# Edge tiles of 128 records in place of 125, their scatters dealt anew over the stages, and four fills issued later

## What is computed

```python
x = x + L0_gnn(xn, edges, type) + L0_mix(xn)      # attention over edges; 4 dense layers of linear attention and ffn
x = x + L0_ffn(layernorm(x))                      # 16 experts, two for each token
x = x + L1_gnn(xn, src, dst, w, w2) + L1_mix(xn)  # below; channel attention
x = x + L1_ffn(xn)                                # the gate picks rows
# in L1_gnn:
a_in  = segment_sum(feat_in[src] * iw[:, None], dst)
a_out = segment_sum(feat_out[dst] * ow[:, None], src)
```

## Time and profile before

| what | us |
|---|---|
| median of 3 runs | 5154.09 |
| lowest and highest run | 5144.35, 5155.28 |
| span of the profiled execution | 5104.5 |
| POOL busy with scatters (L737, 800 of them) | 1684.5 |

### The profile page before, as it was taken

The page is one execution under the profiler, slowest core; times in us unless marked ns, Lnnn a source line. Parts: engine busy times, 40 slices in busy tenths (PEclk is TensorE's granted clock), DMA queues, the critical chain, the costliest instruction groups (busy, mean ns, idle before and its releaser), DMA issues. The chain is left out here.

```text
span 5104.5 us, 67642 instructions
## 1 busy us (share of the span) xinstructions
PE 4208.8 (82%) x19715; PEld 3144.9 (62%) x19715; DVE 3215.8 (63%) x6298; ACT 2149.0 (42%) x7759; POOL 3136.1 (61%) x2100
## 2 busy tenths in 40 slices
PE   6779689889786688888888788469983999999998
PEld 4567467667564466666666566345552788887566
DVE  7667376576386888888888688731114444444447
ACT  2732463473281466666666588312221222222122
POOL 2013388787788777777777688688876445443300
PEclk9989889989898798988888899769996999999999
DMA  9999832332233788888888344449984565563100
GB/s 301 294 336 321 268 67 38 42 63 37 28 61 53 223 265 266 264 267 265 265 266 253 70 94 94 111 105 289 292 246 143 218 236 222 219 234 128 39 15 26
DMA packets 758155, 896.70 MB, mean 176 GB/s; under 512 B 382262, under 2 KB 617430, under 8 KB 754514
## 3 DMA queue, kind: packets, MB, share of 16 engines
q1 hardware_dynamic: 327060, 611.62, 36.0%
q0 software_dynamic: 411376, 263.90, 23.8%
q10 hardware_dynamic: 19406, 17.44, 1.1%
HBM read 668.38 MB, written 222.64 MB: 175 GB/s over the span
## 5 line engine op out<-in xcount | busy, mean ns | idle before, releaser
L737 POOL DMA_INDIRECT pairs<-REC,FARC x800 | 1684.5, 2106 | 619.6 <-DMA pairs<-REC,FARC 231.1
L1102 PE MATMUL a_pa<-a_VW,identf 128*128 128x260 f32 x1760 | 551.3, 468 | 207.9 <-issue 114.2
L994 POOL DMA_INDIRECT a_KV<-kv_tab,KEYS x556 | 536.5, 965 | 173.6 <-issue 159.1
L1102 PEld LDWEIGHTS a_pa<-a_VW,identf 128*128 128x128 f32 x1760 | 389.3, 232 | 289.8 <-issue 121.4
L2664 DVE TENSOR_TENSOR AIN<-AIN,w_pin 128x512 f32<-128x512 f32 (+1 forms) x325 | 216.6, 666 | 374.2 <-PE w_pin L2701 374.0
L1065 ACT ACTIVATE a_VW<-a_KV,a_VW 128x64 f32<-128x64 f32 x1668 | 407.3, 334 | 2.7
L994 POOL DMA_INDIRECT XN<-kv_tab,KEYS x324 | 312.7, 965 | 98.7 <-issue 90.2
L2709 PE MATMUL w_pout<-XN,w_tT 128*128 128x256 f32 x1250 | 318.7, 379 | 0.0
L2678 ACT ACTIVATE w_tT<-w_pt 128x256 f32<-128x256 f32 (+1 forms) x300 | 117.4, 391 | 457.8 <-PE w_pt L2696 456.1
L2599 POOL TENSOR_TENSOR RES<-RES,REC 128x1600 f32<-128x1600 f32 x52 | 188.0, 3631 | 187.6 <-DMA REC<-pairs 187.4
L2599 POOL TENSOR_TENSOR HB<-HB,REC 128x1600 f32<-128x1600 f32 x48 | 174.2, 3642 | 181.4 <-DMA REC<-pairs 181.0
(11 more groups left out here) (661 smaller groups left out, 10066.9 us busy)
## 6 DMA issues: line engine op xcount, KB each, us to landing
pairs<-ZERO SPq DMA_DIRECT2D x32, 5000.0 KB, 46.5
e_W<-in_L_ffn_w SPq DMA_DIRECT2D x192, 512.0 KB, 6.0
REC<-pairs SPq DMA_DIRECT2D x100, 800.0 KB, 8.0
RES<-pairs SPq DMA_DIRECT2D x13, 3200.0 KB
HB<-pairs SPq DMA_DIRECT2D x12, 3200.0 KB, 10.3
m_crow<-cell_tab SPq DMA_DIRECT2D x71, 488.3 KB
row_tab<-a_arow SPq DMA_DIRECT2D x220, 130.0 KB, 4.4
a_tyb<-ty_tab SPq DMA_DIRECT2D x110, 256.0 KB, 7.0
```

Of the source, the lines that this page charges most:

```text
L737: pool.indirect_dma_start(self.pairs[half], bass.IndirectOffsetOnAxis(self.FARC[:, i:i + 1].bitcast(I32), 0), self.REC[:, i, 0:4].bitcast( ...
L994: pool.indirect_dma_start(KV[t % UB][:, j, :], None, self.kv_tab, bass.IndirectOffsetOnAxis(self.SIDX[:, t * ROW + j:t * ROW + j + 1], 0)) ...
L1102: last = pe.matmul(sums[t % NA], self.identf[:, :], VW[:, t % NV, e, :, :], start=e == 0, stop=e == ROW - 1)
```

## The change

- Tiles have 128 records: EP = 128, 781 full columns and a tail of 32 edges in column 782 (EW = 781, EU = 782), padded to EC = 784 columns. The padding points at far cells and weighs zero. 98 merges in place of 100, histogram blocks of 28 columns (14 of them) in place of 40 (10), constants of the comparison and of the far cells to match. Each input is loaded by a DMA for the full columns and one for the tail, the latter after VectorE's memsets of the last columns.
- 782 scatters in place of 800, dealt as layers (32, 130, 260, 210), project 50, nodes 100, experts what is left (2), and none in att_out, route and batch_norm. (As layer 0's loop is written, its 32 come to 30 in both kernels.)
- The first 120 go to table 0 alone, in place of 40.
- In layer 1 the four fills are issued after the wait for cx, the weights and the next front, ahead of the back's cell loads.

```diff
-EP = 125
-EC = E // EP
+EP = P
+EW = E // EP
+EU = -(-E // EP)
+EC = -(-EU // 8) * 8
+FARNODE, FARSRC = 4032, 3199
-BESIDE = (32, 142, 150, 70)
+BESIDE = (32, 130, 260, 210)
-BACKS = ((3, 3, 3, 3, 2), (3, 3, 3, 3, 3), (3, 3, 3, 3, 3), ())
-ALONE = 40
-NODES = 156
-LAST = 14
+BACKS = ((3, 3, 3, 3, 2), (3, 3, 3, 3, 2), (3, 3, 3, 3, 2), ())
+ALONE = 120
+NODES = 100
+LAST = 0
...
-        HC, HL, HH = 40, 64, N // 64 + 1
+        HC, HL, HH = 28, 64, N // 64 + 1
...
+                    for x, empty in ((DI, FARNODE), (SI, FARSRC), (TI, 0)):
+                        dve.memset(x[:, EW:], empty)
+                    dve.memset(WT[:, :, EW:], 0.0).then_inc(s_pad, 1)
...
-                        act.dma_start(dst[0:EP, 0:EC], a[x].rearrange("(p e) -> p e", p=EP)).then_inc(s_in, 16)
+                        act.dma_start(dst[:, 0:EW], a[x][0:EP * EW].rearrange("(p e) -> p e", p=EP)).then_inc(s_in, 16)
+                    act.wait_ge(s_pad, 1)
+                    for dst, x in ((DI, "dst"), (SI, "src"), (TI, "edge_type_64")):
+                        act.dma_start(dst[0:E - EP * EW, EW:EW + 1], a[x][EP * EW:].rearrange("(p e) -> p e", e=1)).then_inc(s_in, 16)
...
-            if self.placed < EC:
+            if self.placed < EU:
...
-                    self.place_pairs(pool, 44)
+                    self.place_pairs(pool, 50)
...
-                    self.place_pairs(pool, 9)
...
-                    self.place_pairs(pool, 12)
...
-                            if layer == 1:
-                                self.fill(sp, 2 * FILL - LATE, 2 * FILL)
...
+                            if layer == 1:
+                                self.fill(sp, 2 * FILL - LATE, 2 * FILL)
...
-                    self.place_pairs(pool, 38)
```

More of the change, by code:

```diff
@@ L406, in open_up @@
         s_oh, s_hs, s_cnt, s_hd = (n(f"q_{x}") for x in ("oh", "hs", "cnt", "hd"))
-        s_p0, s_w1, s_p1, s_bo, s_own = (n(f"q_{x}") for x in ("p0", "w1", "p1", "bo", "own"))
+        s_p0, s_w1, s_p1, s_bo, s_own, s_pad = (n(f"q_{x}") for x in ("p0", "w1", "p1", "bo", "own", "pad"))
         s_cf, s_ct, s_cr, s_cd, s_park, s_rec = (n(f"q_{x}") for x in ("cf", "ct", "cr", "cd", "park", "rec"))
-        HC, HL, HH = 40, 64, N // 64 + 1
+        HC, HL, HH = 28, 64, N // 64 + 1
         NB = EC // (2 * HC)
@@ L449, in _ @@
                     pool.iota(PI[:, :], pattern=[[0, 1]], base=0, channel_multiplier=1).then_inc(s_io, 1)
-                    pool.iota(CPI[:, :], pattern=[[1, 2]], base=249, channel_multiplier=-2).then_inc(s_io, 1)
+                    pool.iota(CPI[:, :], pattern=[[1, 2]], base=490, channel_multiplier=-3).then_inc(s_io, 1)
                     v = self.bd[:, :].rearrange("p (h d) -> p h d", d=32)
@@ L456, in _ @@
                                        base=31, pattern=[[32, P // 32], [0, 32]], channel_multiplier=-1)
-                    pool.memset(self.REC[:, :, 7:8], 2.0 ** 121)
+                    pool.memset(self.REC[:, :, 7:8], 2.0 ** 119)
                     pool.memset(CNT[:, HH:], 0.0)
@@ L477, in _ @@
                     dve.wait_ge(s_io, 5)
-                    dve.tensor_scalar(CPI[:, :], CPI[:, :], 23, None, ALU.logical_shift_left)
+                    dve.tensor_scalar(CPI[:, :], CPI[:, :], 22, None, ALU.logical_shift_left)
                     for j in range(LOW):
@@ L482, in _ @@
                     dve.drain()
-                    dve.tensor_scalar(self.C2[:, :], CPI[:, 0:1].bitcast(F32), 1.5, None, ALU.mult).then_inc(s_cp, 1)
+                    dve.tensor_scalar(self.C2[:, :], CPI[:, 0:1].bitcast(F32), 2.0, None, ALU.mult).then_inc(s_cp, 1)
                     dve.tensor_scalar(SG[:, :], SGI[:, :], -2.0, 1.0, ALU.mult, ALU.add)
@@ L488, in _ @@
                     dve.tensor_tensor(SP[:, 1:], SG[:, 0:LOW - 1], SG[:, 1:], ALU.mult)
-                    dve.wait_ge(s_in, 48)
+                    dve.wait_ge(s_in, 96)
                     live = lambda x: x[0:EP, 0:EC]
@@ L506, in _ @@
                         dve.tensor_tensor(oht[:, b % 2, :, :, :], high.unsqueeze(2).to_broadcast([EP, 2, HH, HC]), ior[:, 0:HH, :].unsqueeze(1).to_broadcast([EP, 2, HH, HC]), ALU.is_equal).then_inc(s_oh, 1)
-                        if b == 2:
+                        if b == 3:
                             dve.wait_ge(x_in, 32)
@@ L512, in _ @@
                             self.finish_stats(dve, st, mean[:, :], var[:, :], NT).then_inc(x_st, 1)
-                        elif b == 3:
+                        elif b == 4:
                             dve.wait_ge(x_sd, 1)
@@ L522, in _ @@
                                                   ALU.subtract, ALU.mult).then_inc(x_xn, 1)
-                        elif b == 5:
+                        elif b == 7:
                             dve.wait_ge(s_p0, 1)
                             dve.tensor_tensor(WR[:, :, :], WT[:, :, :], parts[0], ALU.subtract).then_inc(s_w1, 1)
-                        elif b == 7:
+                        elif b == 10:
                             dve.wait_ge(s_p1, 1)
@@ L574, in _ @@
                     self.load_back(act, 0)
-                    act.wait_ge(s_pin, 32)
+                    act.wait_ge(s_pin, 64)
                     act.activation(parts[0], WT[:, :, :], ACT.Copy).then_inc(s_p0, 1)
@@ L2280, in experts @@
         XU, XR = 4, 8
-        LEFT = EC - self.placed - LAST
+        LEFT = EU - self.placed - LAST
         with ExitStack() as c:
@@ L2479, in _ @@
                 def _(pool):
-                    self.place_pairs(pool, EC - self.placed)
+                    self.place_pairs(pool, EU - self.placed)
                     self.wait_pairs(pool)
@@ L3017, in run @@
         self.ty_tab, self.dl_tab = self.dram("ty_tab", [P * SW], BF16), self.dram("dl_tab", [P * SW // ROW], BF16)
-        self.pairs, self.cell_tab = [self.dram(f"pairs{h}", [CELLS + E, 2]) for h in range(2)], self.dram("cell_tab", [EC, EP])
+        self.pairs, self.cell_tab = [self.dram(f"pairs{h}", [CELLS + EP * EC, 2]) for h in range(2)], self.dram("cell_tab", [EC, EP])
         self.xn_tab = self.dram("xn_tab", [NP, D])
@@ L3024, in run @@
         table = ExitStack()
-        RECS = self.sb(table, "REC", [P, EC, 8], BF16)
-        self.REC, self.FARC = RECS[0:EP, :, :], self.sb(table, "FARC", [EP, EC])
+        RECS = self.sb(table, "REC", [P, NP // 4, 8], BF16)
+        self.REC, self.FARC = RECS[:, 0:EC, :], self.sb(table, "FARC", [EP, EC])
         self.PART = RECS[:, :, :].rearrange("p e j -> p (e j)").bitcast(F32).rearrange("p (b n) -> p b n", b=2)
```

3 lines of the change are left out of this document (2 added, 1 removed).

## The result

The changed kernel takes 5361.66 us in the median (5353.56 to 5375.85), the kernel before 5152.97 beside it: a ratio of 1.0421, 95% interval 1.0396 to 1.0447, 209 us slower. The forecast was 5119, with a range of 5060 to 5240.

A forecast was written before the change was run, and what follows sets the result against it. The prediction saw POOL near its limit, though not alone, in layers 1 to 3, nodes and experts. Its terms, -22 - 20 + 38 - 22 - 7 - 2 = -35, took the median 5154.1 to 5119 us, range 5060 to 5240.

The forecast's parts named there:

- the term of the scatter's price: POOL's scatter of 128 records: busy 0.74 us, period p = 1.04 with issue, between plain DMA and gather.
- +38: Layer 3, 70 scatters become 210: at p = 1.04 the layer takes 218.4 us against 180.7.
- -20: Layer 2, 150 scatters become 260: covered up to p = 1.46, so POOL's tail of 21.4 us goes.
- the other sign that the text named: Prediction also wrong if scatters wait for their table's former pair to land; such waits were 71.3 us in layer 1.
- its bound of 1.21 for the turn: Layer 3: from p = 1.21 on, 210 p - 180.7 reaches the 73 us gained elsewhere.
- The rival with POOL as the bound of the layers: Scatter costs the gather's price or more, POOL bounds layer 3: 5167 at p = 1.27, some 5275 at 1.6; chance 0.21.
- the unchanged price of 2.50: Rival for layers 2 and 3: tiles of 128 leave the scatter's period at 2.50 us, total 5695; chance 0.14.
- Layer 1, -22: Fills moved on SP: VectorE's 27.5 us wait for m_crow goes, 5 charged for later back loads.
- Experts, -22: Experts lose all but 2 scatters; of TensorE's 36.3 us waits for e_XS, 8.0 and 6 stay.
- Opening and layer 0, -7: Tiles of 128: 4 us off the wait for edge types, 3 off layer 0's waits for m_crow.
- Merges, -2: Two merges fewer save some 2.5 us of VectorE each, part of it covered: -2 us.
- stages at 0: Project and nodes not ended by POOL; att_out, route and batch_norm, which lose scatters, covered by VectorE's chain: 0 us.

The follow-up runs named there:

- tiles alone: The changed kernel with the deal, ALONE and place of the fills taken back, so only tiles of 128 stay: 5395.06 against 5542.44 us, ratio 0.9741.
- deal alone: The kernel before with only the new deal and ALONE = 120, tiles still of 125: 6161.36 against 5542.44 us, ratio 1.1119.
- fills alone: The kernel before with the four fills issued after the wait for cx and ALONE left at 40: 5641.65 us, ratio 1.0187.
- first deal by the price: The changed kernel with 140, 170, 76 scatters in layers 1 to 3, 180 in nodes, 14 in batch_norm: 5399.00 us, ratio 0.9747.
- the two fill runs: The kernel before with the four fills after the wait for cx, with ALONE = 40 (5641.65 us, ratio 1.0187) and ALONE = 120 (5660.48, ratio 1.0191).

## Why the prediction was wrong

**The step that failed** is "I take the middle of the plain DMA and the gather, busy 0.74, p = 1.04", the term of the scatter's price. It measured 1.54, and 1.93 to 1.99 apart with the stalls. Put into the prediction's own formula, the layers come out: layer 3 405.1 - 180.7 = +224 in place of +38 (the stage: +227), layer 2 517.1 - 400.5 = +117 in place of -20 (the stage: +116). The waits of pairs for their landing, the other sign that the text named, were 5.7 and 0.6 us in these two layers, so they are not the cause. The mechanism was the one that the text named as deciding, and its bound of 1.21 for the turn, with the cover of 1.46 for layer 2, was passed by far. The rival with POOL as the bound of the layers was the right kind; it was priced up to a period of 1.6, at 5275, and the period of 1.93 to 1.99 lay beyond it, short of the unchanged price of 2.50.

Why the middle was wrong: both ends of it were DMAs that don't add, and the plain write of 128 records shows what the addition costs, 0.57 us. The argument against a low price, that a scatter that adds must read, add and write, stood in the text and got no weight. That POOL's DMAs with a list of 128 cost "at most 1.02" was read from medians and means: single gathers took up to 1.38 us, and a fourth kind, 50 gathers of 0.955, was left out; neither moves the sum. The comparison "125 costs twice what a gather of 128 costs" mixed two differences, the addition and the divisor; only one of them changed. The Trainium skill's rule by the divisor was cited there, for the loads alone; the page gives it for DMAs issued from GpSimd too, and so it bore on the one term that decided, though it has no price.

**Layer 1, -22**: -29 (and -40 between the later profiles). The wait of 27.5 us went, and 12.6 came back where 5 had been charged. But that the stage came out near the forecast is in part luck, for the tiles alone, with the fills still at the head of the queue, make layer 1 397 us long, nearly as short as the changed kernel's 394. VectorE's wait there was:

```profile
DVE m_same L1656 <- DMA m_crow<-cell_tab: 19.8, 1, 19.8
```

Four runs of chip 12 part the two effects. From POOL's first scatter of layer 1 to VectorE's last row it took, in us:

| | fills at the head | fills late |
|---|---|---|
| tiles of 125 | 414.5 (deal alone) | 389.3 (fills alone) |
| tiles of 128 | 393.5 (tiles alone) | 373.5 (first deal by the price) |

The four deals differ too, so this parts them only roughly, and on chip 3 the move took off 14 (416.8 in the kernel before, 403.2 with late fills and ALONE = 120). Still, the move of the fills takes 14 to 25 us off VectorE's time, about as forecast, and the tiles take off another 16 to 21, for which the sum had 2 us of merges. Part of the two together was lost on POOL. The cover of the scatter that needs table 1 held (it is number 122, not 120, and went out at 849.8, long after the fills), but POOL ended the layer 6 us after VectorE, since its pairs waited 137 us for landings. Nine of these waits, from 659 to 745, while the moved fills run, take 4.3 to 8.4 us each, 62 us in all, against 1.7 to 2.7 after the fills:

```profile
692.31 1.54 POOL L747 DMA_INDIRECT pairs<-REC,FARC  x1 [8.21 <-DMA pairs<-REC,FARC]
...
754.90 1.54 POOL L747 DMA_INDIRECT pairs<-REC,FARC  x1 [1.71 <-DMA pairs<-REC,FARC]
```

That the late fills need a long ALONE, and that a long ALONE brings these waits, the two fill runs show.

**Experts, -22**: -38. The mechanism was right, but TensorE's wait for e_XS fell to 6.5, not 14. The first wait was all that stayed. The rest of the gain, some 8 us, goes with TensorE's own busy time, which fell from 387 to 376 us at a granted clock of 0.99 in place of 0.96; the sum had no term for it. The tiles alone give most of it too (9.8 us of such waits with 117 scatters there), as does the deal alone (6.5 us): at 1.84 apart two scatters and a gather fit under a tile, and with hardly any scatters a gather does.

**Opening and layer 0, -7**: -19. The types' wait went from 12.1 to 1.8, so ScalarE's table was not what followed. By the rule of the Trainium skill ("DMA: Bandwidth & Descriptors", "How many engines (k)") both this wait and layer 0's for m_crow should shrink; the first did, by 85%. The second grew in this pair of profiles, 27.9 to 34.9 us, but on chip 12 it is 25.4 and 26.7 us in two kernels of 125 and 21.3 and 20.9 in two of 128, on chip 8 34.5 against 30.7 to 33.6, and on chip 3 29.1 and 38.3 against 36.7, so it shrank on two chips and the third can't say. Layer 0 itself is 13 to 17 us shorter with tiles of 128 on chips 12, 3 and 8, where this pair has 4.

**Merges, -2, and stages at 0**: these can't be told apart from the rest in the layers; in the tiles' run layers 2 and 3 are both shorter than the cover that the prediction took (369 us from POOL's first scatter to VectorE's end in layer 2, not 379, and 160 in layer 3, not 164). Project, nodes and route gained 2 to 5 us each. Batch_norm, counted at 0 with "if it weren't, these would be gains", lost 13 us in the first pair and 4 in the second. The overlap of its subtractions with GpSimd's additions came with the deal, but what it costs differs from one profile to the other, and the tiles alone, with 14 scatters ahead of the additions and subtractions of 419 ns, have a batch_norm of 81 us: there the additions meet VectorE's later steps, two of which take 2504 ns each in place of 288.

**The sum against the median.** The 49.6 us between span and median were taken to lie outside the span. In the changed kernel's profiled execution only 1.7 us do (5368.88 against 5367.2). With as much, the profiled execution of the kernel before took some 5106 us, 38 less than the lowest of its four runs (5144 to 5155), but as much as its runs on chip 2 (5096 to 5119). So it may come from another chip than the runs; the record doesn't say. This leaves the forecast difference as it is, but the first table by stages adds up to 54 us more than the medians show, and its small rows, layer 0's above all, are less sure than the two large ones.

What stays open: layer 0's time goes with the chip (tiles of 128: 391 to 392 us on chips 12 and 2, 405 to 409 on chips 8 and 3 and in the first comparison; tiles of 125: 405 to 406 on chip 12, 422 to 425 on chips 8 and 3, 412 in the first profile), and no run shows why; nor what makes the attention stage long on chips 12, 8 and 3.

## What to carry to other kernels

Before you fill a stage with cheaper work, find the price at which it stops being covered (here 210 p = 180.7 less what the rest gains, p = 1.21), and if no row shows that operation, take the bound on the wrong side of it seriously, not a middle between rows of other operations. Two operations that differ in two ways, as this scatter and gather do, bound nothing between them until one way is held fixed. And when a deal is written by hand, time one part alone: the tiles were worth 147 us, and the deal gave away more than all of it.

## What the hardware showed

- An adding scatter of 127 records of 8 bytes holds POOL 4.70 us, one of 128 1.54, one of 64 1.42, one of 128 without the addition 0.97.
- VectorE's tensor_tensor in fp32 slows when GpSimd runs one at the same time, but not always the same engine: 951 ns in place of 418 in the changed kernel's first profile, while in its second, on chip 8, VectorE kept 425 ns and GpSimd's two additions took 12.87 us in place of 7.37.
- POOL stands idle 1.7 to 2.7 us for the landing of the pair of adding scatters before, and 4.3 to 8.4 while fills of 5 MB run (changed kernel, layer 1).
- The same attention stage took 1153 us in the first profile and 1572 on chip 3, with a granted TensorE clock of 0.88 and 0.75; its gathers kept their price (a median of 946 and 947 ns).
